# Selective scan: every fourth product with the rows of C on GpSimd, with four slots of states and six of rows

## What is computed

```python
dA = jnp.exp(dt[:, :, None] * A)
dBx = (dt * xc)[:, :, None] * Bm[:, None, :]

def step(h, t):
    dA_t, dBx_t, C_t = t
    h = dA_t * h + dBx_t
    return (h, h @ C_t)
_, y = lax.scan(step, jnp.zeros((xc.shape[1], D_STATE), xs.dtype), (dA, dBx, Cm))
```

## Time and profile before

| | us |
|---|---|
| median of 3 runs | 7245.2 (7241.64 to 7256.94) |
| the profiled execution | 7232.93 |
| its span in the trace | 7231.3 |
| of it the stage, first block of channels | about 203, from 2510 to 2712.7 |
| the stage, second block | about 204, from 2712.7 to 2916.7 |

### The profile page before, as it was taken

One profiled execution on the slowest core, in us unless ns is written; L12 is line 12 of the kernel. 1 busy time (PEld: TensorE's weight loads), 2 busy tenths in 40 slices (PEclk: granted clock), 3 DMA queues, 4 the chain that ended last, 5 costly groups with the idle time before them and its releaser, 6 DMA issues. The chain is left out here.

```text
span 7231.3 us, 83961 instructions
## 1 busy us (share of the span) xinstructions
PE 4409.9 (61%) x18990; PEld 2324.8 (32%) x18991; DVE 3986.2 (55%) x6255; ACT 1869.9 (26%) x2810; POOL 2286.6 (32%) x2170
## 2 busy tenths in 40 slices
PE   4888476134997266389656677456775444440586
PEld 2454375111443022275322333223332122220223
DVE  7987375698996599355322333123332112229894
ACT  1476011013884322244201111001111001110352
POOL 0000000500000056200366665666665666650000
PEclk8999687666998587699877888678887666665896
DMA  1471674434664277405555666555666444443442
GB/s 35 153 239 37 221 251 170 143 113 137 181 181 132 101 259 276 151 22 204 182 160 176 189 200 197 156 169 178 196 203 179 137 134 138 137 113 126 141 136 83
DMA packets 465436, 1145.64 MB, mean 158 GB/s; under 512 B 63196, under 2 KB 254068, under 8 KB 452686
## 3 DMA queue, kind: packets, MB, share of 16 engines
q1 hardware_dynamic: 293530, 550.40, 23.6%
q0 software_dynamic: 134816, 447.33, 20.9%
q10 hardware_dynamic: 36996, 146.80, 5.5%
HBM read 885.96 MB, written 261.55 MB: 159 GB/s over the span
## 5 line engine op out<-in xcount | busy, mean ns | idle before, releaser
L2682 POOL DMA_INDIRECT rel1s_rows<-rel_table,rel1s_at x640 | 624.3, 976 | 374.0 <-issue 289.6
L2682 POOL DMA_INDIRECT rel2s_rows<-rel_table,rel2s_at x640 | 616.1, 963 | 373.5 <-issue 220.6
L2682 POOL DMA_INDIRECT rel0s_rows<-rel_table,rel0s_at x640 | 625.2, 977 | 340.7 <-issue 295.6
L2884 PE MATMUL rel2s_acc<-rel2s_rows,rel2s_hot 128*128 x732 | 402.6, 560 | 490.7 <-issue 316.5
L2126 POOL TENSOR_TENSOR mamb_st<-mam_u,mamb_bc 128x1600 f32<-128x1600 f32 x64 | 232.5, 3632 | 1138.2 <-DMA mamb_bc<-dbc 1138.2
L1677 PE MATMUL gatx_acc<-gatx_w,gatx_feat 128*65 128x400 f32 x1600 | 541.6, 501 | 25.1 <-DVE gatx_w L1569 25.1
L2884 PE MATMUL rel1s_acc<-rel1s_rows,rel1s_hot 128*128 x732 | 323.1, 459 | 247.1 <-issue 183.0
L2884 PE MATMUL rel0s_acc<-rel0s_rows,rel0s_hot 128*128 x732 | 324.6, 461 | 240.4 <-issue 161.4
L1569 DVE SCALAR_TENSOR_TENSOR gatx_w<-gatx_w,gatx_adj 128x1600 f32<-128x1600 f32 x200 | 364.0, 1821 | 0.5 <-ACT gatx_w L1625 0.5
L1416 DVE CUSTOM_DVE_ANT_0 gatm_junk<-gatm_srow,gatm_gone 128x3200 bf16<-128x3200 f32 x100 | 343.5, 3490 | 33.4 <-DMA gatm_srow<-gat_scores 29.1
L1677 PE MATMUL latx_acc<-latx_w,latx_feat 128*65 128x400 f32 x800 | 291.9, 509 | 100.7 <-DVE latx_w L1569 100.7
(11 more groups left out here) (613 smaller groups left out, 9418.5 us busy)
## 6 DMA issues: line engine op xcount, KB each, us to landing
mamb_bc<-dbc SPq DMA_DIRECT2D x128, 800.0 KB, 5.8
agg_strip<-strips SPq DMA_DIRECT2D x100, 800.0 KB, 5.8
gatx_adj<-adj SPq DMA_DIRECT2D x200, 400.0 KB, 3.1
adj<-adj_counts SPq DMA_DIRECT2D x25, 1600.0 KB, 7.1
latx_adj<-adj SPq DMA_DIRECT2D x100, 400.0 KB, 3.1
rel_table<-rel0p_prod POOLq DMA_DIRECT2D x25, 1536.0 KB, 6.2
rel_table<-rel0s_prod ACTq DMA_DIRECT2D x25, 1536.0 KB
rel_table<-rel1s_prod ACTq DMA_DIRECT2D x25, 1536.0 KB
```

What stands on the lines that cost most here:

```text
L2682: pool.indirect_dma_start(rows[k][:, u, :], None, table, bass.IndirectOffsetOnAxis(ap=at[:, n:n + 1], axis=0)).then_inc(s_in[u], 16)
L2884: one = nc.tensor.matmul(acc[a][:, :], hots[k], most_two[k], start=fresh and k == 0, stop=False)
```

## The change

RB grows from 4 to 6 and RS from 3 to 4. Of the products with C, those of the steps with q % 4 == 2 (q = 2, 6, ... 30: 8 of 32 in each block of channels) go from DVE to POOL. POOL makes P(q) behind x(q + 1) in its order, and waits ahead of it for scan q, in the first half of the nodes for the copy to `carry` too, and for the C row. A new semaphore `pc` counts these products; PE and the loads of C rows wait for it in place of `s_hc` where the product is POOL's.

```diff
-                    RB, RS = 4, 3
+                    RB, RS = 6, 4
...
+                    s_pc = ph.sem("pc")
+                    by_pool = lambda q: q % 4 == 2
+                    pool_made = lambda q: (q + 2) // 4
+                    dve_made = lambda q: q + 1 - pool_made(q)
+                    multiplied = lambda q: (s_pc, pool_made(q)) if by_pool(q) else (s_hc, dve_made(q))
...
-                                if r >= RB:
-                                    sp.wait_ge(s_hc if m else s_x, (r - RB) // 2 + 1)
+                                if r >= RB and m:
+                                    sp.wait_ge(*multiplied((r - RB) // 2))
+                                elif r >= RB:
+                                    sp.wait_ge(s_x, (r - RB) // 2 + 1)
...
                             nc.gpsimd.tensor_tensor(st[q % RS][:, :], u[:, ct, when(half)], bc[r % RB][:, :], ALU.mult).then_inc(s_x, 1)
+                            if q and by_pool(q - 1):
+                                r = 2 * q - 1
+                                pool.wait_ge(s_h, q)
+                                if q - 1 < S:
+                                    pool.wait_ge(s_kept, q)
+                                pool.wait_ge(s_bc[r % RB], 16 * (r // RB + 1))
+                                nc.gpsimd.tensor_tensor(st[(q - 1) % RS][:, :], st[(q - 1) % RS][:, :], bc[r % RB][:, :], ALU.mult).then_inc(s_pc, 1)
...
+                            if by_pool(q):
+                                continue
                             dve.wait_ge(s_bc[r % RB], 16 * (r // RB + 1))
                             nc.vector.tensor_tensor(tile[:, :], tile[:, :], bc[r % RB][:, :], ALU.mult).then_inc(s_hc, 1)
...
-                            pe.wait_ge(s_hc, q + 1)
+                            pe.wait_ge(*multiplied(q))
```

## The result

| | before | after |
|---|---|---|
| median of 11 runs each, us | 7245.2 (7232.11 to 7257.03) | 7274.17 (7266.26 to 7299.11) |
| ratio after / before, 95% interval | | 1.0046 (1.0036 to 1.0056) |
| the profiled execution's span, us | 7231.3 | 7268.2 |
| scan 0 to scan 31, first block of channels | 183.75 | 201.78 |
| scan 0 to scan 31, second block | 183.74 | 204.80 |

The ratio is +33 us of 7245, with an interval from 26 to 41; the medians lie 29.0 us apart and the two spans 36.9. The forecast was 7283, +37.6.

The account below looks back on a forecast made before the run. The stage goes at DVE's pace, with the resource shared by DVE's and POOL's products nearly as full. Terms 17.5, -0.2 and +1.5 sum to 18.8 us a block, 37.6 in two: 7245.2 + 37.6 = 7283 us, range 7256 to 7303.

Parts of the forecast that it names:

- The exclusion: Two-input SBUF products of DVE and POOL don't run side by side; the later ends behind the first, less 0.14 us.
- the cycle: Four steps, scan 6 to scan 10: 26.45 us in the first half of the nodes, 26.21 in the second.
- The race: POOL's product with B of step 10 starts before DVE's product with C of step 8, which stands 3.2 us.
- Rivals 1 and 2: DVE's product of step 8 goes first in both halves (7237 us, chance 0.13), or the second alone (7260, 0.09).
- rival 4: POOL's in-place product with C costs 4.65 us, 18 us more, 7301; chance 0.06 together with the dear start.
- Rival 5: POOL, back to back, never lets DVE's products in between: some 7 us more a cycle, 7245 + 150; chance 0.01.
- The sum: Per block: 17.5 us for scans 2 to 30, -0.2 at scan 31, 1.5 for last matmuls: 18.8 us.
- The tail: Last two groups of matmuls in a block end 0 to 2.9 us later against scan 31; 1.5 taken.
- The start: Block start costs 0 to 3.2 us, by whether x(3) starts ahead of P(1), hanging on first loads; 0 taken.
- Rival 3: Products don't exclude each other when POOL's is one with C: -17.2 us a block, 7211; chance 0.03.

Follow-up runs that it names:

- The iotas: All POOL products of the stage replaced by iotas that read nothing: changed kernel 6797.93 against 6821.46 us for before, kernel before with the same replacement 6794.78, ratio 0.9957.
- the other chip: The changed kernel, unedited, on a chip where the kernel before takes some 6820 us: 6855.99 against 6821.46 us, ratio 1.0052.

## Why the prediction was right

**The exclusion.** "Whoever starts first keeps its time" was read from two pairs. It held for each product of the cycle above. It also held, within 0.02 us, in all 302 overlaps of a product of DVE with one of POOL that stand as rows of their own in the nine traces with products on POOL: the later one always ends its own 1.82 or 3.56 us, less 0.14, behind the end of the one that started first. The iotas show that it takes more than a busy POOL or a POOL that writes SBUF. The section "Who interferes with whom" of "SBUF — State Buffer" in the Trainium skill says both, that the one to issue first keeps the shared pair and that a GpSimd instruction which only writes doesn't contend with a DVE instruction with two SBUF inputs; the trace agrees in both (4.99 beside a product of 3.56, 1.82 beside an iota of 3.54).

**The race.** It was the narrowest step: x(10) ahead of P(8) by 0.24 us, and by 0.12 in the second half. Measured 0.25 (2569.67 against 2569.92), and for x(18) and P(16) in the second half:

```profile
2622.75 3.55 POOL L2133 TENSOR_TENSOR mamb_st<-mam_u,mamb_bc 128x1600 f32<-128x1600 f32 x1
...
2622.86 5.12 DVE L2175 TENSOR_TENSOR mamb_st<-mamb_st,mamb_bc 128x1600 f32<-128x1600 f32 x1
```

0.11. The forecast was right here by margins that small, on the reading that waits already met cost POOL nothing, as on DVE. That reading was correct: back to back POOL starts some 0.05 us before the last one ends (2564.58 + 5.14 = 2569.72 against 2569.67), with two waits in between. Rivals 1 and 2 fell on this.

**The durations.** P(7) 3.57 forecast, 3.60 measured; P(8) 5.00 and 4.99; P(9) 1.82 and 1.83; POOL's product with C 3.56 and 3.55, which ends rival 4; the cycle 26.45 and 26.53, in the second half 26.21 and 26.23. P(6) began 0.32 us after its scan where I had 0.22, and this is the 0.1 of the first half.

**Rival 5.** DVE did get its turn between two products of POOL: P(7) stood behind x(8) alone, and x(9), queued right behind, was itself put back to 5.14.

**The sum.** +17.3 from scan 0 to 31 was in the forecast of a block (17.5 - 0.2), and 18.0 came. The first block from its scan 0 to the scan 0 of the second took 221.22 against 202.32 us, +18.9 where I had 18.8. Two terms were chosen within bounds. The tail: the last matmuls ended 9.4 us after scan 31 began (2717.30, see below), 8.5 before, +0.9 where I took 1.5. The start: I took 0 of 0 to 3.2. The first block of the changed kernel confirmed it (its P(1) started 0.28 us ahead of x(3)), the second did not. The first two rows below are the end of the first block (for the tail), the other two the start of the second:

```profile
2717.30 3.55 DVE L2166 TENSOR_TENSOR_SCAN mamb_st<-mamb_dA,mamb_carry,mamb_st 128x1600 f32<-128x1600 f32 x1 [1.83 <-ACT mamb_dA L2153]
2719.16 7.50 PE L2187 MATMUL mamb_acc<-mamb_st,g_ident 128*128 128x512 f32 x16 [3.73 <-POOL mamb_st L2140]
...
2746.24 3.56 POOL L2133 TENSOR_TENSOR mamb_st<-mam_u,mamb_bc 128x1600 f32<-128x1600 f32 x1
...
2746.49 4.99 DVE L2175 TENSOR_TENSOR mamb_st<-mamb_st,mamb_bc 128x1600 f32<-128x1600 f32 x1
```

x(3) came 0.25 us ahead of P(1) of the second block and cost it the 3.2 us. On the other chip P(1) of that block started 0.13 us ahead of x(3) and took 1.82, and the stage was 422.54 in place of 426.02. So this race went either way. That it hangs on when the first loads land is the reading of the prediction; no run tested it.

**What was mis-sized.** Rival 3 gave 34 us to the change if POOL's product with C didn't exclude. That credited the change with what lifting the exclusion gives the kernel before just as well: with iotas both gain, and the stages differ by 2.1 us. Even then the moved product is worth only some microseconds, since the next scan waits for its dA anyway: in the changed kernel with iotas the gap between two scans is 1.77 us behind POOL's product and 1.96 behind one of DVE in the first half of the nodes, 1.84 and 1.77 in the second. This doesn't touch the forecast itself.

**Luck, and what is open.** The spans of the two profiled executions differ by 36.9 us, close to the 37.6 of the sum, but two things cancel in that. The stage grew by 40.0, 3.2 of it the product at the start of the second block; and the first scan began 3.0 us earlier than before (2515.52 against 2518.51), in work that the change doesn't touch. In all eleven traces it began between 2515.52 and 2521.58, so this lies within the scatter. The timed runs grew by 33 (26 to 41): 37.6 and 40.0 both lie inside, and the rest is not attributed.

## What to carry to other kernels

Before work moves from DVE to POOL, add up what both do with two SBUF inputs: this sum is a resource of its own, here 21.5 us of 23.8 before and 23.3 after. When it is nearly full, the order within it decides, and here an engine that was given room to run ahead took its turns at the wrong moments. With six slots of rows, one wait that starts POOL's work with DVE's scan gained 21 us (12 to 29), where moving the products lost 33. In this kernel a race between two engines could be called from the trace to 0.1 us where both sides were counted from the same event, while the one at the start of a block, which the prediction had left open, went either way.

## What the runs showed of the hardware

- DVE's product (two inputs in SBUF) beside an iota of POOL, which only writes: 1.82 us, 3.54 us. Beside a product of POOL that started first it took up to 5.14 us. DVE's scan, with one of its two tile inputs in PSUM, was never held: 3.48 to 3.55 us in all eleven traces, also in the second half of the nodes, where it starts from a column of numbers (`carry`) in SBUF.
- Of two overlapping products, one on DVE and one on POOL, the later one ended its own time less 0.14 us behind the first (302 overlaps, all within 0.02 us).
- An instruction of POOL starts 0.03 to 0.05 us before the last ends when its waits are met (2564.58 + 5.14 against 2569.67), and 0.17 us after the end of the DVE product it still waits for (2567.28 against 2565.29 + 1.82).
- The first block of the changed kernel took nearly the same on two chips where the kernel before differs by 6% in its whole time (7245 and 6821 us): 201.78 and 201.49 us from scan 0 to scan 31.
